# Attention with float32r halves of the array, a written order of each step, and eight unused matmuls ahead of its barrier

## The reference

```python
q, k, v = [split_heads(x @ W + b) for W, b in ((Wq, bq), (Wk, bk), (Wv, bv))]   # (4, 16, 1024, 16)
scores = einsum('bhqd,bhkd->bhqk', q, k) / sqrt(16)
scores = where(causal, scores, -inf)
out = einsum('bhqk,bhkd->bhqd', softmax(scores), v)
x = layernorm(x + out @ Wo + bo)
x = layernorm(x + shared_expert(x) + sum_of_top2_experts(x))
```

## Time and profile before

| | |
|---|---|
| time, median of 3 runs | 1043.27 us (1041.78 to 1044.07) |
| span of the profiled execution | 975.7 us |
| outside of the span (median less span) | 67.6 us |
| projection, with the early maxima and the barrier | 118.6 us |
| attention, 15 full steps | 461.1 us, 30.74 us each |
| last attention step and barrier | 28.2 us |
| the rest | 367.8 us |
| PE busy from 149 to 575 us | 420.5 of 426.0 us |
| DVE, ACT, POOL busy in the same stretch | 361.4, 266.6, 77.8 us |

### The profile page before, as it was taken

How to read it: one execution, slowest core, us unless ns; L and a number is a source line. 1 busy time by engine, 2 the same in 40 slices (tenths; PEclk the granted TensorE clock), 3 DMA queues, 4 the chain that set the end, 5 groups by cost and what they waited for, 6 DMA issues and landing times. The chain is left out here.

```text
span 975.7 us, 18404 instructions
## 1 busy us (share of the span) xinstructions
PE 854.0 (88%) x5476; PEld 478.9 (49%) x5477; DVE 660.1 (68%) x1527; ACT 476.2 (49%) x686; POOL 300.0 (31%) x368
## 2 busy tenths in 40 slices
PE   7979799999999989999999997799898999999300
PEld 4635434444444434444444432687556777777200
DVE  6428688888888887888888870489892122466364
ACT  3423266656666656656666566455322444444100
POOL 3423312211112111221112211442477500464373
PEclk9979899999999999999999999889899999999755
DMA  8773855444764266425754000710126745766443
GB/s 285 193 205 131 162 67 75 100 97 59 131 85 89 36 117 118 68 38 106 130 66 57 9 2 25 235 65 23 60 103 210 232 137 152 207 207 211 157 126 95
DMA packets 82464, 113.95 MB, mean 117 GB/s; under 512 B 8945, under 2 KB 60401, under 8 KB 82417
## 3 DMA queue, kind: packets, MB, share of 16 engines
q1 hardware_dynamic: 57808, 78.01, 38.1%
q0 software_dynamic: 6720, 18.88, 5.9%
q10 hardware_dynamic: 17888, 16.41, 5.2%
HBM read 62.55 MB, written 50.33 MB: 116 GB/s over the span
## 5 line engine op out<-in xcount | busy, mean ns | idle before, releaser
L658 ACT ACTIVATE work<-ps 128x1024 f32<-128x1024 f32 (+3 forms) x384 | 293.8, 811 | 185.5 <-PE ps L725 185.3
L335 DVE TENSOR_REDUCE m_neg<-ps 128x1 f32<-128x512 f32 (+3 forms) x432 | 265.6, 662 | 29.2 <-PE ps L320 18.7
L629 POOL TENSOR_SCALAR_AFFINE_SELECT work<-work 128x512 f32<-128x512 f32 x128 | 81.2, 634 | 394.4 <-ACT work L658 390.0
L317 PE MATMUL ps<-stacks 96*128 96x512 bf16 (+3 forms) x528 | 151.9, 332 | 1.5 <-DVE m_neg L335 1.5
L725 PE MATMUL ps<-stacks 99*128 99x512 bf16 (+3 forms) x528 | 124.6, 329 | 6.4 <-PEq L371 4.8
L335 DVE TENSOR_REDUCE m_neg_late<-ps 128x1 f32<-128x384 f32 (+3 forms) x176 | 106.7, 636 | 27.4 <-PE ps L320 27.4
L740 PE MATMUL ps<-work,vg 128*32 128x512 f32 (+3 forms) x1056 | 112.5, 498 | 1.6 <-POOL work L629 1.6
L320 PE MATMUL ps<-mask_b,ident_b 128*128 128x128 bf16 x512 | 100.3, 223 | 0.0
L317 PEld LDWEIGHTS ps<-stacks 96*128 96x128 bf16 x528 | 50.0, 98 | 95.0 <-DVE m_neg L335 48.8
L1243 DVE TENSOR_TENSOR work<-work,ps 128x256 f32<-128x256 f32 x48 | 20.2, 421 | 106.7 <-ACT work L1062 106.7
L1421 PE MATMUL ps<-wgu,work 128*128 x384 | 91.7, 382 | 0.3 <-issue 0.3
(11 more groups left out here) (143 smaller groups left out, 1098.4 us busy)
## 6 DMA issues: line engine op xcount, KB each, us to landing
stacks<-qk_parts SPq DMA_DIRECT2D x132, 128.0 KB, 6.3
qk_parts<-work SPq DMA_DIRECT2D x32, 384.0 KB, 3.0
y_sorted<-work SPq DMA_DIRECT2D x8, 1536.0 KB, 9.9
work<-y_sorted SPq DMA_DIRECT2D x48, 256.0 KB
z_sorted<-work ACTq DMA_DIRECT2D x48, 256.0 KB
wgu<-qk_parts SPq DMA_DIRECT2D x60, 128.0 KB, 6.5
work<-in_xT SPq DMA_DIRECT2D x8, 512.0 KB, 4.8
work<-in_x SPq DMA_DIRECT2D x8, 512.0 KB, 3.6
```

The source lines that it names most:

```text
L317: mm = pe.matmul(dst, qs[r][0:KS, h0 + m, qt * P:(qt + 1) * P], ks[r][0:KS, h0 + m, half * CH:half * CH + w], start=True, stop=not diag)
L335: dve.tensor_reduce(dst, ps[:, bank, 0:heads * w].rearrange("p (h k) -> p h k", h=heads), AX.X, ALU.max, negate=True).then_inc(reduced, 1)
L629: pool.affine_select(out=blk_, in_=blk_, compare_op=ALU.is_ge, fill=0.0, base=0, pattern=[[0, GH], [1, P]], channel_multiplier=-1).then_in ...
L658: act.activation(probs[:, s + 2 * pair:s + 2 * pair + 2, off:CH], ps[:, SCORE_BANK + 2 * pair:SCORE_BANK + 2 * pair + 2, off:CH], ACT.Exp, ...
```

## The change

The attention is written anew around matmuls in `float32r`; the projection hands over other parts; the blocks after it are the same but for where `wgu` and `yT_all` lie in SBUF.

- q and k are split in two parts (high, low) stored as float32 and multiplied as `float32r`. There are three products (high·high, high·low, low·high): 48 rows, and two more for the maximum. Two heads stand in one stack, one in partitions 0 to 49, one in 64 to 113, and the matmuls of the two follow each other, each over its half of the array's rows, into two banks. ACT's `middle` and POOL's `low` are gone. A chunk's store is 2.1 MB instead of 1.57 MB; a stack is still 1.5 MB but comes in 18 DMAs.
- The maxima come in 20 pieces of two banks (two heads side by side, up to 1,024 columns). The causal mask is added by four bfloat16 matmuls of 64 rows for a pair of heads.
- Scores and maxima share one ring of three slots of two banks each (banks 0 to 5). Bank 7 holds the transposes; the early maxima have one slot.
- 11 units instead of 12: the 256-wide and the 128-wide unit of the first half are one.
- The maxima are split in two parts by POOL (two operations, ahead of its masks), not by DVE; DVE keeps the minimum of both halves.
- The order of a step is a written string, `ORDER_OF_STEP`; a weigh comes two units behind its exp, not one.
- PE runs all 16 steps without a loop; ACT's loop holds three steps.
- At the end of the projection PE does eight float32 matmuls whose result nothing reads.

```diff
-PRODUCTS = [(0, 0), (0, 1), (1, 0), (0, 2), (2, 0), (1, 1)]
+PRODUCTS = [(0, 0), (0, 1), (1, 0)]
 KS = len(PRODUCTS) * DK
-KM = KS + 3
-UNITS = [(qc, kt) for qc in range(HALVES) for kt in range(CT * (qc + 1))]
+KM = KS + 2
+ROWS = 64
+PAIRED = GH // 2
+UNITS = [(0, [(0, 0, 0)]), (0, [(1, P, P)]), (0, [(2, 2 * P, 2 * P), (3, 3 * P, P)])]
+UNITS += [(1, [(kt, off, off)]) for kt, off in enumerate([0] * CT + [P * j for j in range(CT)])]
...
-        heads = 4 if w == P else 2 if w == 2 * P else 1
-        MAXES += [(qt, h, heads, half, w) for h in range(0, GH, heads)]
+        heads = 2 if w <= 2 * P else 1
+        MAXES += [(qt, h, heads, half, w) for h in range(0, PAIRED, heads)]
...
-RING = [4, 5, 7]
+SLOTS = 3
+OUT_BANK, TURN_BANK = 6, 7
+WEIGH_BEHIND = 2
+ORDER_OF_STEP = (
+    "m0 s0a m1 s0b w-2 m2 s1a t1 s1b w-1 m3 s2a m4 s2b o1 s3a m5 m6 w0 s3b w1 m7 s4a t0 m8 s4b m9 w2 m10 "
+    "s5a m11 s5b m12 w3 s6a m13 s6b o0 s7a m14 w4 m15 s7b m16 w5 s8a m17 w6 s8b m18 s9a w7 s9b s10a m19 "
+    "w8 s10b"
+)
...
+RING_USERS = [item for item in ORDER if item[0] in ("scores", "max")]
+def slot_bank(item):
+    return 2 * (RING_USERS.index(item) % SLOTS)
...
         def piece_scores(pe, i, r, n, bank):
+            qt, p0, pairs, half, w = MAXES[n]
+            diag = half == qt // CT
+            for m in range(pairs):
+                dst = [ps[:, bank + x, m * w:(m + 1) * w] for x in range(2)]
+                for x in range(2):
+                    rows = slice(x * ROWS, x * ROWS + KS)
+                    mm = pe.matmul(dst[x], qs[r][rows, qt // CT, p0 + m, qt % CT * P:(qt % CT + 1) * P],
+                                   ks[r][rows, p0 + m, half * CH:half * CH + w], start=True, stop=not diag)
                 if diag:
-                    mm = pe.matmul(dst[:, w - P:w], ident_b[:, :], mask_b[:, :], start=False, stop=True)
+                    for j in range(2):
+                        for x in range(2):
+                            rows = slice(x * ROWS, (x + 1) * ROWS)
+                            one, low = (ident_b, mask_b) if j == x else (ident_x, mask_x)
+                            mm = pe.matmul(dst[x][:, w - P + j * ROWS:w], one[rows, :], low[rows, j * ROWS:P],
+                                           start=False, stop=j == 1)
...
+        def max_parts(pool, i, qc):
+            wait_apart(pool, *((m_both, i + 1) if qc else (reduced, NM * i + NM0)), pool_waited)
+            if not (isinstance(i, int) and i == 0):
+                wait_apart(pool, mT_ready[qc], i, pool_waited)
+            pool.tensor_copy(high, m).then_inc(m_step, 1)
+            pool.wait_ge(m_step, done + 1)
+            pool.tensor_tensor(low, m, high.bitcast(F32), ALU.subtract).then_inc(m_ready[qc], 1)
...
                 staggered(pe, [(0, project)], CHUNKS, until=CHUNKS - 4)
+                pe.wait_ge(low_ready[0], CHUNKS)
+                for n in range(FILLERS):
+                    pe.matmul(ps[:, 0, :], wqk[:, 0, 0, 0:P], xt[1][:, 0, :], start=True, stop=True)
...
                 def step(i, r, more=True):
-                    for u in DIAG[:CT]:
-                        mask(i, u)
+                    max_parts(pool, i, 1)
+                    for u in DIAG[:ND0]:
+                        mask(i, r, u)
                     if more:
                         wait_count(pool, pv_done, NU * (i - 1))
                         values(pool, i + 1, (r + 1) % STACKS)
-                    for u in DIAG[CT:]:
-                        mask(i, u)
+                        max_parts(pool, i + 1, 0)
+                    for u in DIAG[ND0:]:
+                        mask(i, r, u)
...
-                def scores(i, r, u, pair):
+                def scores(i, r, u, pair, first, last):
+                    qc, parts = UNITS[u]
+                    bank = slot_bank(("scores", u, pair))
+                    if pair == 0 and u in (0, NU0):
+                        pe.wait_ge(m_loaded[qc], 64 * i + 64)
+                    slot_free(i, ("scores", u, pair), first, last)
+                    for kt, off, at in parts:
+                        for x in range(2):
+                            rows = slice(x * ROWS, x * ROWS + KM)
+                            mm = pe.matmul(ps[:, bank + x, at:at + CH - off], ks[r][rows, pair, kt * P:(kt + 1) * P],
+                                           qs[r][rows, qc, pair, off:CH], start=True, stop=True)
```

More of the change, by code:

```diff
@@ L8 @@
 BF16 = mybir.dt.bfloat16
+F32R = mybir.dt.float32r
 I32 = mybir.dt.int32
@@ L53, with first_column @@
 STACKS = 3
-RING = [4, 5, 7]
-def unit_width(u):
-    qc, kt = UNITS[u]
-    return CH - max(0, P * (kt - CT * qc))
-def attention_order():
-    main = [("scores", 0, 0), ("scores", 0, 1), ("weigh", -1, 0)]
-    for u in range(NU - 1):
-        main += [("scores", u + 1, 0), ("scores", u + 1, 1), ("weigh", u, 0)]
-    cost = [unit_width(u) * (2 if what == "weigh" else 1) for what, u, _ in main]
-    pieces = [m[2] * m[4] + 60 for m in MAXES]
-    order, n, done, spent = [], 0, 0, 0
-    for item, c in zip(main, cost):
-        order.append(item)
-        if item == ("scores", 1, 1):
-            order.append(("turn_max", 1, 0))
-        if item == ("weigh", 1, 0):
-            order.append(("turn_out", 1, 0))
-        if item == ("weigh", 5, 0):
-            order.append(("turn_out", 0, 0))
-        done += c
-        while n < NM and (spent + pieces[n] / 2) / sum(pieces) <= done / sum(cost):
-            order.append(("max", n, 0))
-            spent += pieces[n]
-            n += 1
-            if n == NM0 + TURN_AFTER:
-                order.append(("turn_max", 0, 0))
-    assert n == NM
+SLOTS = 3
+OUT_BANK, TURN_BANK = 6, 7
+def first_column(u):
+    return min(at for _, _, at in UNITS[u][1])
+WEIGH_BEHIND = 2
[4 more added lines that the diff above has]
+)
+def attention_order():
+    what = {"s": "scores", "m": "max", "w": "weigh", "t": "turn_max", "o": "turn_out"}
+    order = []
+    for word in ORDER_OF_STEP.split():
+        pair = "ab".index(word[-1]) if word[0] == "s" else 0
+        order.append((what[word[0]], int(word[1:].rstrip("ab")), pair))
+    assert sorted(n for w, n, _ in order if w == "max") == list(range(NM))
+    assert sorted(n for w, n, _ in order if w == "weigh") == list(range(-WEIGH_BEHIND, NU - WEIGH_BEHIND))
     return order
@@ L107, in present, with slot_before @@
     return not (first and item == ("turn_out", 1, 0))
-def ring_before(item, first, last, second=False):
-    at = RING_USERS.index(item) - len(RING)
+def slot_before(item, first, last):
+    at = RING_USERS.index(item) - SLOTS
     while at >= 0:
@@ L115, in ring_before, with turn_before @@
             return RING_USERS[at], 0
-        at -= len(RING)
+        at -= SLOTS
     if first:
         return None, 0
-    at += len(RING_USERS)
-    while not present(RING_USERS[at], second, False):
-        at -= len(RING)
-    return RING_USERS[at], 1
+    return RING_USERS[at + len(RING_USERS)], 1
+def turn_before(item, first, last, second=False):
+    at = TURNS.index(item) - 1
+    while at >= 0:
+        if present(TURNS[at], first, last):
+            return TURNS[at], 0
+        at -= 1
+    if first:
+        return None, 0
+    at += len(TURNS)
+    while not present(TURNS[at], second, False):
+        at -= 1
+    return TURNS[at], 1
 EARLY = [("max", n) for n in range(NM)]
 EARLY.insert(NM0 + TURN_AFTER, ("turn_max", 0))
-EARLY_BANKS = [6, 7]
+EARLY_BANK = 6
+FILLERS = 8
 EARLY_CHUNKS = 3
@@ L694, in step @@
                 def step(i, first=False, last=False):
-                    max_parts(dve, i, 1)
+                    both_halves(dve, i)
                     for item in ORDER:
                         what, n, _ = item
-                        if item not in RING_USERS or not present(item, first, last):
+                        if what in ("scores", "weigh") or not present(item, first, last):
                             continue
                         if what == "max":
-                            piece_maximum(dve, i + 1, n, ring_bank(item))
-                            if n == NM0 - 1:
-                                max_parts(dve, i + 1, 0)
+                            piece_maximum(dve, i + 1, n, slot_bank(item))
                         elif what == "turn_max":
-                            copy_maxima(dve, i + 1 - n, n, ring_bank(item))
+                            copy_maxima(dve, i + 1 - n, n, TURN_BANK)
                         else:
```

311 lines of the change are left out of this document (153 added, 158 removed).

## The result

The changed kernel takes 1101.11 us (median of 4 runs, 1099.09 to 1102.24) where the kernel before takes 1043.17 beside it: a ratio of 1.055, 95% interval 1.052 to 1.058. I had forecast 1005, faster. It is slower by 5.5%.

A forecast was written before the change was run, and what follows sets the result against it. PE alone bounded the attention before; after, PE, DVE and ACT meet in one ring. 122.5 + 15 x 28.2 + 24.5 = 570.0 for 607.9, so span 937.8 and time 1005; forecast 980 to 1030, range 950 to 1060.

The forecast's parts named there:

- start of the attention: Ahead of the attention: eight unused matmuls make PE late at the barrier; start 122.5 instead of 118.6, +3.9 (0 to +6).
- a step at a clock of 1.00: Attention step: PE, DVE and ACT meet in one ring; DVE 22.6 us plus idle 4.7 to 5.9; 28.2 taken.
- falls of the clock: PE's granted clock: only the first 30.4 us, at 0.92 before, were considered; counted 0 to -1 us, taken as 0.
- last step and tail: Last step, no maxima: exp 17.4 us, then mask, two weighs, copy, transpose, normalise and barrier about 7; 24.5 instead of 28.2.
- outside of the span: Whole kernel: the profiled span stands 67.6 us under the median of the runs, so a span of 937.8 becomes 1005.
- cheap end: PE's step: float32r in one pass, two halves side by side; scores and maxima 3.9 + 3.9, sum 21.5 us.
- The idle time before m7: DVE in each step, 1.5 us: s3b needs s3a's slot, and exp s3a needs the probability slot that w0 frees.
- The halves: Scores and maxima on PE: matmuls on two row halves overlap at least in part; at the cheap end they take half.
- A: The 48 pairs of a step: halves don't overlap, 7.8 us of PE, step about 33.2, 1080 us; chance 0.12.
- C: PE's matmuls: float32r priced as float32, PE 44.6 us, a step 46, kernel 1270; chance 0.04.
- D: Attention step: DVE is the only bound, its idle falls to 2 us, a step of 24.6, kernel 950; chance 0.11.
- B: PE's weight loads: 0.15 us or more, one after another; PE 28, a step 31.5, about 1055 us; chance 0.08.

The follow-up runs named there:

- the kernel before with gaps: Kernel before, with TensorE also waiting for the exp of units 0 and 1 after it has filled them; 1118.64 us, ratio 1.072.
- both moves: Changed kernel with t1 moved ahead of w-2 and w0 moved ahead of s3a in the written order; 1031.42 us, ratio 0.987.
- w0 early: Changed kernel with w0 moved from behind m6 to ahead of s3a; 1036.38 us, ratio 0.994 to the kernel before.
- The transpose early: Changed kernel with t1 moved from behind s1a to ahead of w-2; 991.10 us beside the kernel before at 982.57, ratio 1.011.
- two matmuls in the wait: Changed kernel with two unread float32 matmuls of 512 columns ahead of s3a's wait for the row maxima; 1002.74 us beside 982.57, ratio 1.022.

## Why it stays cold: are the rows in use enough?

**Two unread matmuls in the second gap only** (between w0 and s3b, into the bank of the transposes, steps 2 to 14).

> The changed kernel with two unread float32 matmuls of 512 columns between w0 and s3b in steps 2 to 14, so that of the two idle stretches (1.16 us ahead of s3a, 1.23 us ahead of s3b) only the first is left; the unread ones write the bank of the transposes. Theory X (it takes both, close together): granted clock 1.00 in steps 2 to 14, each 31.2 to 31.8 us, 36 to 42 us under the changed kernel. Theory Y (the first idle stretch alone is enough): the clock falls to 0.50 as before in about 9 of 15 steps, steps of 31 and 37 mixed, and the time is that of the changed kernel within 1%, or above it.

**Four of them behind s3b, both gaps left.**
```diff
                             scores(i, r, n, pair, first, last)
+                            if item == ("scores", NU0, 1) and 2 <= i <= STEPS - 2:
+                                turn_free(i, ("turn_max", 0, 0), first, last, second)
+                                for _ in range(4):
+                                    pe.matmul(ps[:, TURN_BANK, :], wqk[:, 0, 0, 0:P],
+                                              wqk[:, 0].rearrange("p c n -> p (c n)"), start=True, stop=True)
```


> The changed kernel with both idle stretches left as they are and four unread float32 matmuls of 512 columns and the whole array (3.5 us of work) behind s3b in steps 2 to 14. It asks what ends the cold stretch, which lasts 12 to 16 us in a cold step of the changed kernel though TensorE is then busy in all of each 2 us. Theory (full-array work without a pause brings the clock back, as in the kernel before with gaps, where it was back 3 to 4 us after the gap): the cold stretch is under 8 us, a cold step takes 31.2 + 4 to 6, about 36, a warm one 33 to 34. Rival (the clock comes back after a time of its own, whatever runs): cold stretches of 12 us or more, a cold step of 40 us or more, and the kernel 30 us or more slower than the changed one.

**The kernel before with gaps, on few rows**, and then **without the gaps**:
```diff
-                mm = pe.matmul(dst, qs[r][0:KS, h0 + m, qt * P:(qt + 1) * P],
-                               ks[r][0:KS, h0 + m, ...
+                mm = pe.matmul(dst, qs[r][0:48, h0 + m, qt * P:(qt + 1) * P],
+                               ks[r][0:48, h0 + m, ...
-                        mm = pe.matmul(..., ks[r][0:KM, h, ...], qs[r][0:KM, h, ...]
+                        mm = pe.matmul(..., ks[r][64:KM, h, ...], qs[r][64:KM, h, ...]
```


> The kernel before with the two waits of TensorE (as in the run with gaps), and with all score matmuls on 35 rows and all maxima matmuls on 48 rows instead of 99 and 96, of the same columns and in the same order; so the scores lack the first four products, the maxima the last three, and what is computed is not attention. Theory (rows in use do not matter to the granted clock): steps as in the run with gaps, 33 to 36 us and 41 in every third, mean clock of the steps 0.92. Rival (few rows in use keep the clock down longer): the mean clock of the steps is 0.85 or less, and steps of 36 us or more are the rule.

> The kernel before, all of its waits as they were and no gap added, with all score matmuls on 35 rows and all maxima matmuls on 48 rows instead of 99 and 96 (so what it computes is not attention). With gaps added and these few rows, steps took 44 to 57 us at a granted clock of 0.50 to 0.76; with gaps and all rows 33 to 41 us at 0.83 to 1.00. Theory (few rows do nothing by themselves, they only keep a fallen clock down): apart from the first step or two the clock is 1.00 and a step takes 30.4 us. Rival (few rows lower the clock by themselves): the mean clock of the steps is under 0.9 throughout, with steps of 33 us or more and TensorE busy for over 95% of them.

Steps of the last two, first with gaps, then without:
```profile
526.41:573.34 46.93, 44.42 (x242) 14.04 (x241) 27.19 (x53) 19.63 (x27) 5.63 (x9) 0.68 0.36 67
573.34:630.73 57.39, 55.05 (x242) 14.94 (x241) 27.85 (x53) 19.73 (x27) 5.63 (x9) 0.50 0.24 28
```
```profile
128.09:170.49 42.40, 42.17 (x237) 12.93 (x236) 26.63 (x51) 19.48 (x27) 5.66 (x9) 0.70 0.30 39
...
284.17:338.77 54.60, 54.60 (x242) 14.82 (x241) 27.88 (x53) 19.75 (x27) 5.66 (x9) 0.50 0.25 31
```
With gaps and few rows (1318 us, one run) the steps take 41.4 to 57.4 us at 0.50 to 0.83, so the rival held. The run without gaps (1382 us, one run) was the most telling. It is the kernel before, no gap added, the same number of matmuls of the same columns in the same order: by the records TensorE is busy for 54.60 of 54.60 us, in twelve such steps in a row, and its clock stands at 0.50 from 213.4 to 926.8 us. With 96 and 99 rows it was at 1.00. My theory that few rows only keep a fallen clock down was wrong: the clock was back at 1.00 from 152 to 169 us and fell to 0.50 again, with 0.23 us of recorded idle time in between.

Yet the edit changed more than the number of rows. The scores now use rows 64 to 98 and the maxima rows 0 to 47, and the masks still use all 128; the values multiplied are other ones as well. In the run without gaps, at a clock of 1.00:
```profile
197.36 0.28 PE L317 MATMUL ps<-wgu 48*128 48x256 bf16 x1
197.57 0.23 PE L320 MATMUL ps<-mask_b,ident_b 128*128 128x128 bf16 x1
197.73 0.39 PE L725 MATMUL ps<-stacks 35*128 35x512 bf16 x1
197.74 0.39 PE L317 MATMUL ps<-wgu 48*128 48x512 bf16 x1
```
Two matmuls of 512 columns on different rows now start 0.01 us apart, and from a mask to the next matmul it takes 0.16 us instead of 0.05 (302.81 to 302.86 in the earlier trace rows). That time counts as busy. So the clock may have fallen for the fewer rows, or for such pauses inside what the records call busy; no run has the one without the other. What is shown is that a busy share of 100% in the records does not hold the clock up: how much the array does in that time counts too.

The Trainium skill ("TensorE: Matmul & The Clock Gate", "HAM oscillation") puts the lower level down to waits in which the engine is idle, and its Part 1 has activity release it. That waits lower the clock, the kernel before with gaps shows. The run without gaps fell with 0.23 us of recorded idle time in the 17 before, and stayed down for 713 us of recorded activity, which neither covers. As far as the records show the pauses, the run differs from both, and the measurement decides.

The fills fit a clock that full-array work brings back. With only the second gap filled (against 1042.29 us: 1085.96, ratio 1.043, 1.040 to 1.046) the first gap still lowers the clock, in 7 of the 13 filled steps, but for 3 us or so: 33.4 us at 0.95 instead of 37 at 0.77. That is neither of my two theories. With full-array work behind the gaps (1133.23, 1.089, 1.084 to 1.094, as it adds work everywhere) the same fall ends within 7 us in four of six cold steps and within 10 in two. The cold steps take 37.3 to 39.1 us (I had 36), the warm ones 34.8, as the added work costs 3.6 us in each. Slices of one cold step, then the unread matmuls themselves:
```profile
268.00:270.00 2.00, 1.50 (x14) 0.76 (x18) 0.93 (x2) 0.00 (x0) 1.42 (x2) 0.83 0.18 46
...
274.00:276.00 2.00, 2.00 (x3) 0.81 (x3) 0.00 (x0) 0.77 (x1) 0.00 (x0) 0.50 0.49 131
276.00:278.00 2.00, 2.00 (x6) 0.76 (x4) 0.00 (x0) 0.00 (x0) 0.00 (x0) 0.96 0.77 131
...
273.63 4.94 PE L815 MATMUL ps<-wqk 128*128 128x512 f32 x8
```

**The first step.** With both moves it was cold with no idle stretch over 0.45 us before: between 123.5 and 129.8 us TensorE had matmuls of 48, 50 and 64 rows and one small transpose. As there is no step before it, its w-2 and w-1 are missing; two unread full-array matmuls went into the place of each, with and without the eight of the projection.
```diff
                             elif not first:
                                 weigh(i - 1, (r - 1) % STACKS, NU + n)
+                            else:
+                                for _ in range(2):
+                                    pe.matmul(ps[:, OUT_BANK, :], wqk[:, 0, 0, 0:P], ...)
```


> Both moves (w0 ahead of s3a, the maxima's transpose ahead of w-2), and in the first step alone two unread float32 matmuls of 512 columns and the whole array in the place of each of the two weighs that are not there (w-2, w-1). Without these four the clock fell to 0.50 from 127.8 to beyond 146 us, with TensorE idle for no more than 0.45 us before, though from 123.5 to 129.8 it ran nothing but matmuls of 48, 50 and 64 rows. Theory R (what counts is also how much of the array is in use): the clock stays at 1.00 in the first step, which takes 29.4 to 31 us instead of 35.0, and the attention ends at 603 to 605 instead of 608.0; the kernel is 1.5 to 2.0% faster than the kernel before. Rival (only idle time counts; the fall came from the wait at the barrier): the first step stays at a clock near 0.71 and takes 35 to 37 us.

> As the kernel with both moves and the four unread matmuls of the first step, without the eight unused ones ahead of the barrier. Without either, the attention began at 119.7 and the first step took 35.6 us at a clock of 0.68. Theory (the four alone bring the clock back, the eight only delay): first step 30 to 33 us, attention's end at 600 to 603, 2 to 4 us under the kernel that has the eight as well. Rival (TensorE comes cold out of the 4.1 us of waiting and needs the eight to keep its clock): first step 34 us or more, end at 605 or later.

```profile
125.34:156.80 31.46, 28.77 (x256) 13.05 (x255) 23.06 (x26) 19.22 (x24) 6.44 (x12) 1.00 0.25 52
```
```profile
122.26:155.76 33.50, 30.79 (x256) 13.68 (x255) 22.99 (x26) 19.16 (x23) 6.48 (x12) 0.94 0.33 49
```
Four matmuls turn a first step of 35.04 us at 0.71 into one of 31.46 at 1.00; the output projection begins at 604.3 instead of 608.0 (the "end" of the expectations). Without the eight TensorE comes cold out of the barrier (0.50 from 120 to 126), but the four bring it back, and it begins at 603.5: the eight are not needed. Against 1041.33 us: 1034.13 (0.991, 0.988 to 0.995) and 1033.45 (0.991, 0.987 to 0.994). I had expected 1.5 to 2.0% for the first. That is no better a ratio than the 0.987 (0.982 to 0.993) of the two moves alone; the intervals overlap, and the gain of some 4 us in the trace is under what these runs can tell. The kernels with both moves are about 1% faster than the kernel before and 6% faster than the changed one.

## Why the prediction was wrong, point by point

From the sum 122.5 + 15 x 28.2 + 24.5 = 570.0, the attention was to end at 570.0; it ended at 668.4. The first four rows are these 98.4 us; the last one lies behind them:

| term | forecast | measured | share of the miss |
|---|---|---|---|
| start of the attention | 122.5 | 122.9 | 0.4 |
| a step at a clock of 1.00, x15 | 28.2 | 31.16 | 44.4 |
| falls of the clock | 0 | 41.8 | 41.8 |
| last step and tail | 24.5 | 36.3 | 11.8 |
| the rest, with what was "outside of the span" | 435.4 | 432.7 | -2.7 |

Two steps of the sum failed, the clock and TensorE's step at full clock, by about as much. Either alone would have made the kernel slower. By the table, without the falls the kernel would take some 1059 us (1101.1 - 41.8), and with steps of 28.2 and the same falls some 1057 (1101.1 - 44.4); both are estimates, and both are over 1043.

**The clock (the first step that failed).** I took the granted clock of 1.00 over to the new kernel, and counted only the first 30 us at 0 to -1. "A granted clock under 1.00 inside the attention" stood in the list of what would make it wrong, without a price, a chance or a rival. Yet the change takes TensorE from 98.7% busy to a step where I myself had it at 21.5 to 24.2 of 28.2 us, and halves the rows of each matmul. Either should have made a rival: a third of a 30-us step spent at half the clock is up to 5 us, twice the whole margin of 2.5 us a step.

**The step at full clock (the second step that failed).** I priced TensorE at 21.5 to 24.2 us of a step and took the middle. It is busy for 27.05 and idle for 4.1 of 31.16. From start to start in that step (229.56 to 260.72), idle time left out:

| TensorE, us a step | forecast | changed kernel | kernel before, 244.46 to 274.82 |
|---|---|---|---|
| scores and maxima | 7.8 to 10.6 | 13.3 | 16.8 |
| masks | 1.4 | 2.6 | 2.3 |
| weighs | 10.4 | 9.3 | 9.4 |
| transposes | 1.3 | 1.8 | 1.6 |

So scores and maxima fell from 16.8 to 13.3 and not to half. My cheap end for a pair of 512 columns was 0.22 us. In the warm steps it takes 0.27 (median) between other pairs, and 0.33 to 0.34 where a weigh or a transpose stands next to it; I had 0.5 us a step for all such changes. Whether they or the weight loads cost it, no run separates. With 27.05 us of TensorE a step of 28.2 leaves 1.2 for its waits, and even with w0 early it waits for 2.1.

DVE was to be busy for 22.6 and idle for 4.7 to 5.9. It is busy for 23.64 and idle for 7.5: changed kernel, DVE at the places that I had named.
```profile
235.22 2.36 DVE L361 TENSOR_REDUCE m_neg<-ps 128x2 f32<-128x1024 f32 x2 [1.07 <-PE ps L347]
239.47 1.23 DVE L361 TENSOR_REDUCE m_neg<-ps 128x2 f32<-128x1024 f32 x1 [1.90 <-PE ps L340]
...
256.62 1.23 DVE L361 TENSOR_REDUCE m_late<-ps 128x2 f32<-128x1024 f32 x1 [0.81 <-PE ps L347]
```
The idle time before m7 (239.47) is 1.90 where I had 1.5; the last five pieces lose 2.7 and m0 to m3 with o1 1.3, both as forecast. What the prediction has no price for is the landing: after DVE's copy of the transposed maxima (230.18 + 0.27) four DMAs go out, and s3a starts at 234.34, 3.9 us behind the copy. It shows as 1.07 us at m5 and, I think, as part of the 1.90 at m7. With w0 early, that wait is filled and the one ahead of s3b goes, and the step is 29.4: the two together were worth 1.7 of the 3.0 us. The transpose early, which shortens the first alone, gives 30.1, so 1.0. How the other 1.3 divide between TensorE's 27.05 and DVE's 1.0 us more, no run shows.

**The halves.** Right in kind, and the point of most doubt: the rows of the two halves do overlap. The two matmuls of a pair start 3 ns apart (median). Changed kernel, from pair to pair:
```profile
146.67 0.50 PE L755 MATMUL ps<-stacks 50*128 50x512 f32 x2
147.01 0.40 PE L340 MATMUL ps<-stacks 48*128 48x512 f32 x2
147.25 0.49 PE L755 MATMUL ps<-stacks 50*128 50x512 f32 x2
```
Two matmuls of 512 columns each take 0.24 us together here, and 0.34 in the pair before, right behind a weigh (I had 0.22 for both). At its best a pair in float32r thus costs about what one bfloat16 matmul did (0.22). Rivals A and C were wrong, and so was D (its step of 24.6 was reached in no run). B's mechanism, loads of 0.15 us one after another, does not show (a 128-wide pair takes 0.11 to 0.17 in all), but its sizes, 28 us of TensorE and a step of 31.5, are close to the 27.05 and 31.16 measured. The right mechanism for a pair did not give the right price for the step.

**The start.** Right: TensorE was the last at the barrier because of the eight matmuls, 122.9 against 122.5.

**The last step and tail.** Forecast 24.5 from ACT's exp and a tail of 7. From its first score it takes 34.7. ACT is busy for 19.5 of the last 33.1 us (row 635.32 above); for the rest it mostly waits for TensorE, whose mean clock is 0.76. Even with the clock at 1.00 in all but 3.4 us of it (two matmuls in the wait) it takes 32.8 from its first score, with ACT idle for 12 us, 4.5 of them in one wait for w0. I had summed the exp and a tail and left out the written order, in which exp and weighs wait for each other; how much of the 10 us over the forecast that is, no run took apart.

**Outside of the span.** Right in sum for the wrong reason. In every other run the span is only 1 to 3 us under the time. The 67.6 us are a difference between sets of runs: the kernel before took 983 us (median) in one set and 1041 to 1045 in the others, and the stage after the attention took 366 to 370 us in the profiles of the first sort (367.8) and 427 to 436 in those of the second, whatever the kernel. The profile shown of before is of the first sort, the times are of the second. Whether the chip makes the difference is open: the set of 983 us and one of 1042 us are both recorded for chip number 5.

## What to carry to other kernels

Price a matmul on part of the rows by its neighbours, too: the pair of 0.24 us took 0.34 beside work of the whole array. TensorE's time saved is also activity taken from it: when a change makes its matmuls thinner or leaves it waiting, price the step once more at the lower clock, and make it a case with a chance. Place the full-array work of a step (here the weighs) so that no stretch is left with thin matmuls and waits alone; where none is at hand, a few unread matmuls may pay, as in the wait for the maxima and in the first step. And put nothing that needs a freshly computed DMA right behind it: 3.9 us from copy to use were more than the order had in hand.

## What the hardware showed that I had not expected

- TensorE busy without a break in the records, and at its lower clock, for 713 us: matmuls of 35 and 48 rows between masks of 128, 54.60 us a step instead of 30.4.
- A clock that fell in the changed kernel with one wait of 1.14 us close behind it, and stayed down for 17 us; with 3.5 us' worth of full-array work behind the same gaps it was back within 7, or 10.
- Two sorts of execution 60 us apart, by the traces all of it in the last stage, which has the indirect DMAs; why is open.
- Not settled: in the changed kernel thin matmuls and idle time come together, and no run there separates the one from the other. For the kernel before it is shown that the clock falls without recorded waits, not whether the rows do it or the pauses between unlike matmuls that the records count as busy. Nor is it settled why some steps of the changed kernel stay at 1.00 with the same gaps.
